# Moving 32 of 128 column copies from GpSimd to ScalarE ahead of its first silu of the last stage, and GpSimd's first roots from column 96 to column 80

## The chip, the cores and the metric

One core of one Trainium2 chip runs the whole program. The metric is device time in microseconds (us) of one execution. The kernel before takes 555.73 us (median of three runs, 555.04 to 556.38). The execution that was profiled took 554.09 us; its trace spans 552.1 us.

Engines in the rows: PE is TensorE's matmul, PEld its weight load, DVE is VectorE, ACT is ScalarE, POOL is GpSimd, SP is SyncE; a q behind a name is the sequencer of that engine, which handles registers, loads and waits.

## The reference

`x` is (64, 64, 256), 4096 tokens of 256 features. Two layers are applied and the result is added to `x`.

```python
# layer 1: mixture of 4 experts with a shared one, over all tokens c = L0(x, cond)
h = gelu(context_c @ ew1[e] + eb1[e]);  y = h @ ew2[e] + eb2[e]
out = out + w_be[:, e] * mask[e] * y          # plus the shared expert
# layer 2, on c, called x here
x1 = x @ sw1.T + sb1;  x2 = x @ sw2.T + sb2
sh = _ln(silu(x1) * x2, s_ln_g, s_ln_b)       # over H = 128
shared_out = sh @ sw3.T + sb3                 # all 4096 tokens
x_moe = x[index_b, index_t]                   # 512 selected positions
expert_scores = sigmoid(x_moe @ eg_w.T + eg_b)
top1_idx = argmax(expert_scores + exp_bias)
h1, h2 = x_moe @ ew1[e] + eb1[e], x_moe @ ew2[e] + eb2[e]     # 8 experts
z = _ln(silu(h1) * h2, sel_ln_g, sel_ln_b)
final_out = shared_out.at[index_b, index_t].set(shared_w * shared_out[...] + expert_w * expert_out)
```

The indices name fewer than 128 distinct tokens here, so they fit into one group, and only that group is worked on.

## The kernel before

**Layer 1** fills the first 480 us and keeps PE busy. Its sums lie in SBUF in `acc`, features in the partitions, a token in a column (two halves of 128 features, so a token is 128 partitions by 2 elements). When the last sum is written, VectorE raises `summed_all` (at 479.6 us in the trace).

**The last stage** (functions `stage2_*`) works through eight pieces of 512 tokens, k = 0 to 7, and one group of 128 selected tokens, the "group" below. Per piece:

- ScalarE `c_high(k)`: the sums cast to fp16 (L505). VectorE `c_low(k)`: the rest of them (L751).
- PE `first(k)`: 12 matmuls, x1 and x2 (L614). ScalarE `silu(k)` (L511), VectorE `gated(k)` (L758), ScalarE `g_high(k)` (L525), VectorE `g_low(k)` (L763).
- PE `centre(k)`: takes the mean off (L627). ScalarE `square(k)`: sums of squares (L517), which raises `sq_ready`.
- the root 1/sqrt(variance + eps): for pieces 0 to 3 on GpSimd, two pieces at a time, `roots(0)` and `roots(1)`, 15 dependent small operations each (L972 to L979), which raise `var_taken`. `roots(0)` waits for `square(1)`, `roots(1)` for `square(3)`.
- PE `second(k)`: the product with sw3 (L640). VectorE `rows(k)`: scales it by the root and adds x (L778); it waits for `var_taken` and raises `row_done`.

PE's order is first(0), a last part of layer 1 (`output_late(1)`, 487.73 to 493.13 us), then first(k), centre(k-1), and from k = 4 on second(k-4). `second(1)` waits for both halves of `rows(0)`, since they read the banks that it writes.

**The group.** GpSimd copies 128 columns of `acc`, chosen by a table of indices in SBUF (`ctab`), to `cgT`: one load of 16 registers, then 16 copies of 128x2 elements (`copies`, L947), eight times. The first three loads are done ahead of `summed_all`. The first of `roots` stands between column 95 and column 96, the second behind column 127. The last copy raises `cg_pool`. PE waits for it in `router(0)` (L647), which stands behind first(6), and runs the group's first matmuls (`gfirst`, L656) behind that.

Each engine runs its own list in the order written; semaphores tie them together. Nothing is reordered at run time.

Of the kernel before, what the change touches and what calls it, by code (L numbers as in the profile page):

```python
# [29 lines left out]
ACT = mybir.ActivationFunctionType  # L30
# [3 lines left out]
P = 128  # L34
# [25 lines left out]
COLS = NB * BS + SLOTS * SEG + 6  # L60
# [5 lines left out]
ROUND = 12582912.0  # L66
NJ = FE + 1
NL = 2
WARM = 11
NS1 = NS - NL  # L70
MGX = MG + 1
# [13 lines left out]
def program(nc, a):  # L85
    with ExitStack() as ctx:
# [3 lines left out]
        def sem(name):  # L90
            return ctx.enter_context(nc.semaphore(name))
# [229 lines left out]
        def take(base, lo, shape, dt=F32):  # L321

            n = 1
            for s in shape:
                n *= s
            words = n if dt is not F16 else n // 2
            v = base[:, lo:lo + words]
            if dt is not F32:
                v = v.bitcast(dt)
            names = "abc"[:len(shape)]  # L330
            if len(shape) == 1:
                return v
            return v.rearrange(f"p ({' '.join(names)}) -> p {' '.join(names)}",
                               **{c: s for c, s in zip(names, shape)})
# [8 lines left out]
        cgT = take(SW, 9216, [DB, P])  # L343
# [12 lines left out]
        ctab = stf[0:1, 0:MX].bitcast(I32)  # L356
# [25 lines left out]
        misc_in, w3s_in, ce8_in, xg_in = sem("misc_in"), sem("w3s_in"), sem("ce8_in"), sem("xg_in")  # L382
# [5 lines left out]
        var_taken, gvar_taken = sem("var_taken"), sem("gvar_taken")  # L388
        u_done, row_done, out_done, scat_done = sem("u_done"), sem("row_done"), sem("out_done"), sem("scat_done")

        cg_pool, fwr_in, late_done = sem("cg_pool"), sem("fwr_in"), sem("late_done")
        root_made, groot_made, root_step = sem("root_made"), sem("groot_made"), sem("root_step")
        logit_ready = sem("logit_ready")
# [38 lines left out]
        def halves(k, part):  # L432
            return chl[:, k % CR, part * DB:(part + 1) * DB, :].rearrange("p d (b t) -> p d b t", t=NT)

        def column(at):
            return acc[:, :, bass.ds(at, 1)]
# [61 lines left out]
        def stage2_act(act):  # L498

            def c_high(k):  # L500
                if k == NQ - 1:
                    act.wait_ge(late_done, 2)
                if k >= CR:
                    act.wait_ge(ab_done[1], k - CR + 1)
                nc.scalar.activation(halves(k, 0), summed(k), ACT.Copy).then_inc(c_hi, 1)  # L505
# [52 lines left out]
            def groot(g):  # L558
                act.wait_ge(gvar_taken, g + 1)
                nc.scalar.activation(tmg, tmg, ACT.Sqrt).then_inc(groot_made, 1)  # L560

            act.wait_ge(summed_all, 1)
            c_high(0)
            c_high(1)
            for k in range(NQ):
                silu(k)
                if k + 2 < NQ:
                    c_high(k + 2)
                if k == 6:
                    gsilu(0, 0)  # L570
                if k >= 1:
                    square(k - 1)
                g_high(k)
                if k == 6:
                    gsilu(0, 1)
                    score(0)
                    gsilu(0, 2)
                    gsilu(0, 3)
                if k == 7:
                    mix(0)  # L580
                    gsilu(0, 4)
# [19 lines left out]
        def stage2_pe(pe, output_late):  # L601
# [41 lines left out]

            def router(g):
                pe.wait_ge(cg_pool, g + 1)
                for db in range(DB):
                    pe.matmul(ps1[2][:, P:P + 9], cgT[:, db, :], rwr[:, db, :],  # L647
                              start=(db == 0), stop=(db == DB - 1))
# [282 lines left out]
        def stage2_pool(pool, link):  # L931
            pool.wait_ge(rows_ready, 1)
            link(nc.gpsimd.tensor_scalar(Cm32, ident[:, :], -1.0 / FH, None, ALU.add))
            link(nc.gpsimd.tensor_copy(Cm, Cm32))
            nc.gpsimd.memset(epss, EPS * WS * WS)
            nc.gpsimd.iota(io8, pattern=[[1, FE]], base=-FE, channel_multiplier=0,
                           allow_small_or_imprecise_dtypes=True).then_inc(const2_ready, 1)
            regs = [pool.alloc_register(f"pool_column{j}") for j in range(48)]
            groups = pool.value_load(tab[0:1, NR * ROW + 2:NR * ROW + 3], min_val=1, max_val=MGX)

            def addresses(g, at, j):
                pool.load(regs[j:j + 16], ctab[0:1, g * P + at:g * P + at + 16])  # L942
                return [pool.snap(x, min_val=0, max_val=COLS - 1) for x in regs[j:j + 16]]

            def copies(at, cols):
                for j, col in enumerate(cols):
                    i = nc.gpsimd.tensor_copy(cgT[:, :, at + j:at + j + 1], column(col))  # L947
                return i

            def x_rows(g):  # L950
                nc.gpsimd.indirect_dma_start(
                    out=xg, out_offset=None, in_=a["xR"],
                    in_offset=bass.IndirectOffsetOnAxis(ap=gid[:, g:g + 1], axis=0)).then_inc(xg_in, 16)

            def gather(g):
                x_rows(g)
                for at in range(0, P, 16):
                    i = copies(at, addresses(g, at, 0))
                i.then_inc(cg_pool, 1)

            def roots(q):
                taken = [q * 14]

                def link(i):
                    taken[0] += 1
                    i.then_inc(root_step, 1)
                    pool.wait_ge(root_step, taken[0])

                pool.wait_ge(sq_ready, 2 * q + 2)
                two = slice(2 * q * MG, (2 * q + 2) * MG)  # L970
                out = rstd[:, two]
                link(nc.gpsimd.tensor_scalar(tms, sums2[:, two], 1.0 / FH, EPS, ALU.mult, ALU.add))  # L972
                link(nc.gpsimd.tensor_scalar(out.bitcast(I32), tms.bitcast(I32), -0.5, MAGIC, ALU.mult, ALU.add))
                for n in range(3):
                    link(nc.gpsimd.tensor_tensor(qms, out, out, ALU.mult))
                    link(nc.gpsimd.tensor_tensor(qms, qms, tms, ALU.mult))
                    link(nc.gpsimd.tensor_scalar(qms, qms, -0.5, 1.5, ALU.mult, ALU.add))
                    link(nc.gpsimd.tensor_tensor(out, qms, out, ALU.mult))
                nc.gpsimd.tensor_scalar(out, out, 1.0 / WS, None, ALU.mult).then_inc(var_taken, 1)  # L979

            def scatter(g):

                pool.wait_ge(moe_ready, g + 1)
                nc.gpsimd.indirect_dma_start(
                    out=a["out"], out_offset=bass.IndirectOffsetOnAxis(ap=sid[:, g:g + 1], axis=0),
                    in_=moe, in_offset=None, bounds_check=TOK - 1, oob_is_err=False).then_inc(scat_done, 16)
                pool.wait_ge(scat_done, 16 * (g + 1))

            def group_in_front():
                pool.wait_ge(misc_in, 4 * 16)  # L990
                ahead = [addresses(0, at, at) for at in (0, 16, 32)]
                pool.wait_ge(summed_all, 1)
                for n in range(3):
                    copies(n * 16, ahead[n])
                for at in range(48, P, 16):
                    if at == 96:
                        roots(0)
                    i = copies(at, addresses(0, at, 0))
                i.then_inc(cg_pool, 1)
                roots(1)  # L1000
                x_rows(0)
                pool.wait_ge(out_done, 16 * NH)
                scatter(0)

            def groups_behind(g):
                gather(g)
                scatter(g)
                if g + 1 < MGX:
                    with pool.If(groups > g + 1):
                        groups_behind(g + 1)  # L1010

            with pool.If(groups > 1):
                group_in_front()
                groups_behind(1)
            with pool.If(groups < 2):
                group_in_front()
# [178 lines left out]
        def _(pe):  # L1195
# [48 lines left out]
            pe.wait_ge(zeros_ready, 1)  # L1244
            for n in range(WARM):
                pe.matmul(pst[:, :], zeros[:, 0:P], zeros, start=True, stop=True)
# [149 lines left out]
            def hidden_late(n):  # L1396
                at = 1 + TOK - (NL - n) * CH
                hidden(late + n, SH, lambda xp, db: X[:, 2 * xp + db, at:at + CH])
# [12 lines left out]
        def _(dve):  # L1411
# [376 lines left out]
            def late_store(n):  # L1788

                dve.wait_ge(y_done, last + (R0 + 2 + n))  # L1790
                at = NB - (NL - n) * CB
                for db in range(DB):
# [160 lines left out]
```

## Time and profile before

| | us |
|---|---|
| median of three runs | 555.73 (555.04 to 556.38) |
| profiled execution | 554.09 |
| its span in the trace | 552.1 |
| PE busy | 539.6 (98% of the span) |
| VectorE busy | 396.9 |
| ScalarE busy | 261.9 |
| GpSimd busy | 177.3 |

The busy share says that PE is the engine to look at; it doesn't say where PE waits. The chain of work that ended last is followed back from the last instruction; where it leaves PE for another engine, PE was waiting. The list of waits names for a stretch who waited for whom. The timeline shows an engine's work in order, with the idle time ahead of a piece in brackets and what ended it.

### The profile page before, as it was taken

Reading aid. Unit: us, or ns where it says so; the run is one execution under the profiler, and the core shown is the slowest. Engines: PE = TensorE matmul, PEld = TensorE weight load, DVE = VectorE, ACT = ScalarE, POOL = GpSimd, SP = SyncE. Lnnn points to the kernel's source line nnn. Section 1 sums busy time; section 2 is a strip of 40 time slices with the busy share of each in tenths; the row PEclk is TensorE's granted clock in tenths of the full one; section 3 lists DMA queues with packets and bytes.
Section 4 is the critical chain, followed back from the end, with each engine's and each line's share of the span. In section 5 each row is a group of like instructions: output and inputs, shape, how many; then the busy total and the mean of one; then the engine's idle time right before and its main releaser. Section 6 shows DMA issues by size and latency. Waiting matters only on the chain.

```text
span 552.1 us, 16532 instructions
## 1 busy us (share of the span) xinstructions
PE 539.6 (98%) x5082; PEld 481.1 (87%) x5083; DVE 396.9 (72%) x1046; ACT 261.9 (47%) x632; POOL 177.3 (32%) x566
## 2 busy tenths in 40 slices
PE   8999999999999999999999999999999999999895
PEld 5888888886889999999999999999999999865774
DVE  5979988674975757677675684887786645767585
ACT  6665766751434444343443433434424434539470
POOL 0280000000464523535335243342242410298700
PEclk9999999999999999999999999999999999999999
DMA  7722245300100002323310000000000000192233
GB/s 262 257 113 67 86 152 152 96 2 4 37 1 3 2 2 78 116 79 119 113 78 3 2 2 1 3 2 2 3 4 3 2 5 4 47 365 80 87 121 115
DMA packets 28476, 36.88 MB, mean 67 GB/s; under 512 B 4762, under 2 KB 24115, under 8 KB 28132
## 3 DMA queue, kind: packets, MB, share of 16 engines
q1 hardware_dynamic: 28292, 35.57, 19.6%
q8 instruction: 47, 0.77, 0.6%
q14 instruction: 41, 0.34, 0.2%
q0 software_dynamic: 96, 0.20, 0.1%
HBM read 27.30 MB, written 8.53 MB: 65 GB/s over the span
## 4 chain that ended last, share of the span: by engine, by line
PE 87%; POOL 4%; issue 3%; DVE 2%; POOLq 1%; DMA 1%; SPq 1%; ACT 0%; DVEq 0%; ACTq 0%
PE ps_out L1240 41%; PE ps_hidden L1210 40%; POOL W L947 2%; PE ps_hidden L656 2%; DMA W<-in_xT 1%; PE ps_out L1289 1%; DVE hbuf L1444 1%; PE ps_turn L640 0%; POOLq L942 0%; PE ps_hidden L640 0%; SPq L1021 0%; PE ps_small L640 0%; PE ps_hidden L614 0%; DVE W L1427 0%; PE ps_out L678 0%
## 5 line engine op out<-in xcount | busy, mean ns | idle before, releaser
L1240 PE MATMUL ps_out<-hbuf,W 128*128 128x242 f16 (+4 forms) x2304 | 242.9, 266 | 0.5 <-DVE W L1427 0.5
L1240 PEld LDWEIGHTS ps_out<-hbuf,W 128*128 (+1 forms) x2304 | 218.3, 98 | 17.5 <-DVE W L1427 0.8
L1074 ACT ACTIVATE h<-ps_hidden,b 128x242 f32<-128x242 f32 (+3 forms) x384 | 151.9, 462 | 67.3 <-PE ps_hidden L1210 64.5
L1882 POOL COPY xs<-X 128x88 f16 x334 | 111.1, 381 | 174.6 <-PE ps_hidden L1210 169.4
L1210 PE MATMUL ps_hidden<-xs,W 128*128 128x242 f16 (+2 forms) x1536 | 156.1, 262 | 1.1 <-issue 1.1
L1210 PEld LDWEIGHTS ps_hidden<-xs,W 128*128 (+1 forms) x1536 | 143.3, 98 | 9.3 <-issue 1.6
L1444 DVE TENSOR_TENSOR hbuf<-h,hbuf 128x484 f16<-128x484 f32 (+4 forms) x192 | 127.5, 664 | 7.5
L1735 DVE SCALAR_TENSOR_TENSOR acc<-ytmp,wrow,acc 128x44 f32 (+1 forms) x334 | 62.9, 260 | 80.5 <-ACT ytmp L1164 69.4
L1442 DVE CAST hbuf<-h 128x484 f16<-128x484 f32 (+4 forms) x192 | 83.8, 436 | 13.9 <-ACT h L1074 12.7
L1210 PE MATMUL ps_hidden<-X,W 128*128 128x256 f16 (+1 forms) x768 | 87.1, 273 | 0.9 <-DVE W L1427 0.8
L1164 ACT ACTIVATE ytmp<-ps_out,b 128x242 f32<-128x242 f32 (+3 forms) x64 | 25.5, 450 | 124.2 <-PE ps_out L1240 124.2
L1210 PEld LDWEIGHTS ps_hidden<-X,W 128*128 128x128 f16 x768 | 74.8, 98 | 11.0 <-DVE W L1427 1.6
L947 POOL COPY W<-acc 128x2 f32 x128 | 26.8, 274 | 37.9 <-DVE f L1803 35.3
L1858 POOL CAST ytmp<-tab 1x385 f32<-1x385 int32 x1 | 0.6, 631 | 102.1 <-DVE tab L1608 102.1
L1083 ACT ACTIVATE acc<-ps_out,b 128x256 f32<-128x256 f32 x28 | 11.7, 469 | 39.8 <-PE ps_out L1240 39.8
L1093 ACT ACTIVATE W<-stage 128x1024 f16<-128x1024 f32 x16 | 17.0, 1061 | 14.5 <-DMA stage<-in_ew 14.5
L1450 DVE SCALAR_TENSOR_TENSOR W<-stage,W 128x1024 f16<-128x1024 f32 x16 | 19.2, 1220 | 5.3 <-ACT W L1093 5.2
L614 PE MATMUL ps_hidden<-W,F 128*128 128x512 f16 x96 | 22.2, 379 | 0.2 <-DVE W L751 0.2
L614 PEld LDWEIGHTS ps_hidden<-W,F 128*128 128x128 f16 x96 | 9.2, 98 | 10.0 <-DVE W L751 0.7
L511 ACT ACTIVATE W<-ps_hidden,fb 128x512 f32<-128x512 f32 x8 | 5.6, 694 | 10.6 <-PE ps_hidden L614 10.6
L1466 DVE TENSOR_REDUCE acc<-W 128x16 f32<-128x336 f32 (+1 forms) x24 | 10.3, 499 | 0.0
L517 ACT ACTIVATE W<-ps_out 128x128 f32<-128x128 f32 x32 | 8.4, 277 | 3.1 <-PE ps_out L627 2.9
(316 smaller groups left out, 298.4 us busy)
## 6 DMA issues: line engine op xcount, KB each, us to landing
stage<-in_ew SPq DMA_DIRECT2D x16, 512.0 KB, 3.9
stage<-in_xR SPq DMA_DIRECT2D x8, 512.0 KB, 3.9
moved_rows<-stage SPq DMA_DIRECT2D x8, 512.0 KB, 2.6
X<-moved_rows SPq DMA_DIRECT2D x8, 512.0 KB, 10.1
out_rows<-X SPq DMA_DIRECT2D x16, 256.0 KB, 2.2
W<-in_xT SPq DMA_DIRECT2D x7, 512.0 KB, 9.3
W<-in_fw SPq DMA_DIRECT2D x1, 2304.0 KB, 11.6
W<-in_sw SPq DMA_DIRECT2D x4, 256.0 KB, 3.6
```

Of the source, the lines that this page charges most:

```text
L614: mm = pe.matmul(ps1[which][:, :], fw(wp, which, db), chl[:, k % CR, 2 * xp + db, :], start=(n == 0), stop=(n == 5))
L947: i = nc.gpsimd.tensor_copy(cgT[:, :, at + j:at + j + 1], column(col))
L1074: i = nc.scalar.activation(h32[:, j, k * size:(k + 1) * size], ps1[j][:, k * size:(k + 1) * size], ACT.Gelu_apprx_tanh, bias=b1[:, bass.ds ...
L1093: nc.scalar.activation(W[:, bass.ds(e * WE + at, 1024)], stage[:, k % 2, :], ACT.Copy, scale=WS).then_inc(hi_ready, 1)
L1164: i = nc.scalar.activation(ytmp[:, bass.ds(parity, 1), db, 0:size].rearrange("p o c -> p (o c)"), psy2[:, bass.ds(parity, 1), db * size:(d ...
L1210: mm = pe.matmul(out, w1(e, wp, db, hb), rhs(xp, db), start=(n == 0), stop=(n == 5))
L1240: mm = pe.matmul(out, w2(e, wp, hb, db), h, start=(n == 0), stop=(n == 3 * HB - 1))
L1442: nc.vector.tensor_copy(hi, src).then_inc(h_hi, 1)
L1444: nc.vector.tensor_tensor(lo, src, hi, ALU.subtract).then_inc(h_ready, 1)
L1450: nc.vector.scalar_tensor_tensor(W[:, bass.ds(e * WE + (at + 2048), 1024)], stage[:, k % 2, :], WS, W[:, bass.ds(e * WE + at, 1024)], ALU. ...
L1735: i = nc.vector.scalar_tensor_tensor(at, y, wrow[:, bass.ds(weight + j, 1)], at, ALU.mult, ALU.add)
L1882: i = nc.gpsimd.tensor_copy(xs[:, parity, :, j * SEG:(j + 1) * SEG], X[:, :, bass.ds(cols[j], SEG)])
```

## The change

ScalarE gets two blocks behind `c_high(1)` and ahead of `silu(0)`: each loads 16 indices to registers and copies 16 columns, 96 to 127 in all; the last copy raises a new semaphore `cg_act`. PE's `router` waits for it too. GpSimd's loop ends at column 95, and `roots(0)` stands ahead of column 80 instead of 96.

```diff
+ACOLS = 32
+        cg_act = sem("cg_act")
@@ stage2_act
+            act.wait_ge(misc_in, 4 * 16)
+            cols = [act.alloc_register(f"act_column{j}") for j in range(16)]
             act.wait_ge(summed_all, 1)
             c_high(0)
             c_high(1)
+            for at in range(P - ACOLS, P, 16):
+                act.load(cols, ctab[0:1, at:at + 16])
+                for j, x in enumerate(cols):
+                    col = act.snap(x, min_val=0, max_val=COLS - 1)
+                    i = nc.scalar.activation(cgT[:, :, at + j:at + j + 1], column(col), ACT.Copy)
+            i.then_inc(cg_act, 1)
             for k in range(NQ):
                 silu(k)
@@ stage2_pe, router(g)
                 pe.wait_ge(cg_pool, g + 1)
+                pe.wait_ge(cg_act, 1)
@@ stage2_pool, group_in_front
-                for at in range(48, P, 16):
-                    if at == 96:
+                for at in range(48, P - ACOLS, 16):
+                    if at == 80:
                         roots(0)
                     i = copies(at, addresses(0, at, 0))
                 i.then_inc(cg_pool, 1)
```

ScalarE before, at the start of the last stage: L505 is `c_high`, L511 `silu`, L525 `g_high`.

```order
L505 ACTIVATE W<-acc 128x1024 [waits summed_all]
L505 ACTIVATE W<-acc 128x1024
L511 ACT_TABLE_LOAD
L511 ACTIVATE W<-ps_hidden,fb 128x512 [waits a_done]
L505 ACTIVATE W<-acc 128x1024
L525 ACTIVATE W<-W 128x512 [waits g_made]
```

ScalarE now, at the same place: L507 is `c_high`, L570 the load of 16 registers, L572 a register operation, L573 the copy of a column, L513 `silu`.

```order
L507 ACTIVATE W<-acc 128x1024
L570 TENSOR_LOAD stage
L572 ISA
L573 ACTIVATE W<-acc 128x2
...
L570 TENSOR_LOAD stage
L572 ISA
L573 ACTIVATE W<-acc 128x2
...
L573 ACTIVATE W<-acc 128x2
L513 ACT_TABLE_LOAD
L513 ACTIVATE W<-ps_hidden,fb 128x512 [waits a_done]
```

Two loads and 32 copies stand between `c_high(1)` and the table load of `silu(0)`, which were neighbours.

GpSimd before, from column 80 to the second roots: L942 is the load of 16 registers, L947 the copy, L972 to L979 a set of roots.

```order
L942 TENSOR_LOAD stage
L943 ISA x2
L947 COPY W<-acc 128x2
...
L972 TENSOR_SCALAR stage<-stage 128x8 [waits sq_ready]
L973 TENSOR_SCALAR stage<-stage 128x8 [waits root_step]
...
L979 TENSOR_SCALAR stage<-stage 128x8 [waits root_step]
L942 TENSOR_LOAD stage
...
L942 TENSOR_LOAD stage
...
L972 TENSOR_SCALAR stage<-stage 128x8 [waits sq_ready]
```

GpSimd now, from column 64 to the second roots: L953 is the load, L958 the copy, L983 to L990 a set of roots.

```order
L953 TENSOR_LOAD stage
L954 ISA x2
L958 COPY W<-acc 128x2
...
L983 TENSOR_SCALAR stage<-stage 128x8 [waits sq_ready]
L984 TENSOR_SCALAR stage<-stage 128x8 [waits root_step]
...
L990 TENSOR_SCALAR stage<-stage 128x8 [waits root_step]
L953 TENSOR_LOAD stage
...
L983 TENSOR_SCALAR stage<-stage 128x8 [waits sq_ready]
```

The first roots come 16 columns sooner, and one load with 16 copies stands between the two sets of roots instead of two loads with 32.

## Rows read from the trace of the kernel before

**Rows 1.** The page: TensorE's granted clock in 40 slices; the chain that ended last, by engine.

```profile
PEclk9999999999999999999999999999999999999999
PE 87%; POOL 4%; issue 3%; DVE 2%; POOLq 1%; DMA 1%; SPq 1%; ACT 0%; DVEq 0%; ACTq 0%
```

**Rows 2.** Waits, 484 to 520 us: who waited for whom; us in total, times, longest.

```profile
DVE X L778 <- POOL stage L979: 1.7, 1, 1.7
...
PE ps_turn L640 <- DVE X L778: 1.4, 1, 1.4
...
PE ps_hidden L647 <- POOL W L947: 1.0, 1, 1.0
```

**Rows 3.** Timeline of PE: start, us, engine, line, operation, out<-in, count, idle before.

```profile
495.56 0.61 PE L627 MATMUL ps_out<-stage,W 128*128 128x128 f16 x8
...
509.22 0.61 PE L627 MATMUL ps_out<-stage,W 128*128 128x128 f16 x8
511.28 0.83 PE L640 MATMUL ps_turn<-V,W 128*128 128x256 f16 x6 [1.45 <-DVE X L778]
...
516.37 0.58 PE L647 MATMUL ps_hidden<-stage,W 128*128 128x9 f32 x4 [1.01 <-POOL W L947]
```

**Rows 4.** Timeline of POOL, from column 64 to the end of the second roots.

```profile
495.37 6.99 POOL L947 COPY W<-acc 128x2 f32 x32 [1.20 <-issue]
...
502.72 1.19 POOL L973 TENSOR_SCALAR stage<-stage 128x8 int32<-128x8 int32 x1
...
509.18 0.24 POOL L979 TENSOR_SCALAR stage<-stage 128x8 f32<-128x8 f32 x1
510.69 5.54 POOL L947 COPY W<-acc 128x2 f32 x32 [1.27 <-issue]
...
520.25 0.23 POOL L979 TENSOR_SCALAR stage<-stage 128x8 f32<-128x8 f32 x1
```

**Rows 5.** Timeline of ACT at the start of the last stage, and the end of square(1).

```profile
480.44 2.00 ACT L505 ACTIVATE W<-acc 128x1024 f16<-128x1024 f32 x2
482.46 1.28 ACT L511 ACT_TABLE_LOAD   x1
486.63 0.69 ACT L511 ACTIVATE W<-ps_hidden,fb 128x512 f32<-128x512 f32 x1 [2.89 <-PE ps_hidden L614]
...
494.46 0.69 ACT L511 ACTIVATE W<-ps_hidden,fb 128x512 f32<-128x512 f32 x1 [5.03 <-PE ps_hidden L614]
...
500.23 0.22 ACT L517 ACTIVATION_READ_ACCUMULATOR W<-ps_out 128x1 f32 x1
```

**Rows 6.** Groups by line and shape, ACT: count, busy us, mean ns, idle before.

```profile
L505 ACT ACTIVATE W<-acc 128x1024 f16<-128x1024 f32 x8 | 8.4, 1061 | 0.0
...
L555 ACT ACTIVATE stage<-stage 128x8 f32<-128x8 f32 x2 | 0.6, 312 | 0.0
...
L541 ACT ACTIVATE stage<-stage 128x1 f32<-128x1 f32 x1 | 0.2, 188 | 0.0
```

**Rows 7.** Timeline of ACT in layer 1: a pair whose addresses come from registers.

```profile
455.34 0.82 ACT L1074 ACTIVATE h<-ps_hidden,b 128x242 f32<-128x242 f32 x2 [0.42 <-PE ps_hidden L1210]
```

**Rows 8.** Timeline of POOL, one block of 16 copies that nothing holds up.

```profile
492.16 2.02 POOL L947 COPY W<-acc 128x2 f32 x16
```

**Rows 9.** By line, register loads: 16 values on POOL, one on ACT; ns min/median/max.

```profile
L942 POOLq TENSOR_LOAD <-stage x8: 1049/1056/1341, 447.5 to 512.4; - x8
L1156 ACTq TENSOR_LOAD <-tab x5: 272/277/279, 444.4 to 469.3; - x5
```

**Rows 10.** Timeline of DVE: the late store, a c_low, a g_low, rows(0).

```profile
493.26 0.76 DVE L1795 SCALAR_TENSOR_TENSOR acc<-ps_out,acc 128x256 f32<-128x256 f32 x2 [2.74 <-PE ps_out L1240]
...
502.63 1.22 DVE L751 TENSOR_TENSOR W<-acc,W 128x1024 f16<-128x1024 f32 x1
...
507.22 0.69 DVE L763 SCALAR_TENSOR_TENSOR W<-W 128x512 f16<-128x512 f32 x1 [0.26 <-ACT W L525]
509.56 0.88 DVE L778 SCALAR_TENSOR_TENSOR X<-ps_turn,stage,X 128x256 f32<-128x256 f32 x2 [1.66 <-POOL stage L979]
```

**Rows 11.** Copies of GpSimd (L947) in a stretch: its length, busy us and count.

```profile
479.70:498.80 19.10, 17.68 (x80) 1.00 0.94 330
```

## The prediction

> **What bounds the kernel now.** I read the chain that ended last first. It is PE for 87% of the span, at a full granted clock in every slice [rows 1], so what counts is where PE stands still in the last stage. The waits of that stretch come second: PE is idle twice for other engines, 1.4 us ahead of second(1), for rows(0), and 1.0 us ahead of the router, for GpSimd's copies; rows(0) itself waited 1.7 us for the roots [rows 2]. Third, the timelines say how the two hang together. PE has issued centre(4) by about 509.8 and starts second(1) at 511.28, idle 1.45; it starts the router at 516.37, idle 1.01 [rows 3]. GpSimd copies columns 64 to 95 until 502.36, works on the first roots until 509.42, waits 1.27 us for a register load, copies 96 to 127 until 516.23, and PE goes on 0.14 us later [rows 4]. So GpSimd sets PE's pace twice in the stretch from 509.8 to 516.4, by 2.46 us in all. ScalarE has its idle time elsewhere: 2.89 us ahead of silu(0) and 5.03 us ahead of silu(1), since PE is busy with the last part of layer 1 there [rows 5].
>
> **What the 32 copies cost ScalarE.** No row shows a 128x2 ACTIVATE. Bounds per copy: the shortest one, 128x1, takes 0.188 us, and two c_highs take 2.00 us where one takes 1.061, so neighbours overlap by 0.12; that leaves 0.07 us of spacing at best. The other end is an ACTIVATE of 128x8 at 0.312 with no overlap [rows 5, 6]. Register addresses don't forbid overlap: a pair of 242 columns with such addresses takes 0.82 us together [rows 7]. GpSimd's 16 copies, with the same register operation between them, take 2.02 us; less the last one's 0.19 that is 0.122 each, a rate set by its sequencer [rows 8]. ScalarE's sequencer has the same pairs to issue, so I take 0.12: 32 x 0.12 = 3.9 us, between 2.2 and 10.0.
>
> Register loads: 16 values take 1.056 us on GpSimd, one value 0.277 on ScalarE [rows 9]; a block of GpSimd that isn't ahead of its load idles 1.20 us [rows 4]. The first load of ScalarE can run under c_high(0) and (1), which need no sequencer; the second is exposed. I take 1.2 us, between 0 and 2.5. Sum: 5.1 us, between 2.2 and 12.5.
>
> ScalarE is free for them at about 482.4 [rows 5]. They end at 487.5; the table load of 1.28 us comes behind them and no longer beside the wait, so silu(0) starts at 488.8 instead of 486.63, 2.2 us late.
>
> What is queued behind: c_high(2), done 1.64 us after silu(0) starts; then on VectorE c_low(2), 1.22, g_low(0), 0.69, and the late store, 0.76 [rows 10]. That is 4.4 us, and PE wants the last two for centre(0) at 495.56 [rows 3]. So silu(0) may start as late as 491.1 at no cost. With 488.8 there are 2.3 us to spare; silu(1) at 494.46 waits for PE as before. If that cover were gone, each microsecond would count in full, because from then on square, g_high, g_low and centre wait for each other in turn. Cost taken: 0.
>
> A rule of the Trainium skill speaks against this step. "ScalarE: Activation LUTs", section "Rules for kernel authors", budgets about 0.3 us for each ACTIVATE; 32 would be 9.6 us, and silu(0) at 494.5, past the limit. The same page, section "What ACT_TABLE_LOAD costs", gives 186 ns for one with immediate scale and bias and an overlap of 93 ns, so some 3.0 us for 32. The 0.188 us row agrees with the second.
>
> **What it gives GpSimd.** 80 columns are copied by 498.80 [rows 11]. Then the roots wait for square(1), whose last read ends at 500.45 [rows 5], so they start at 500.5 instead of 502.4: 1.9 us sooner and not 3.5. They took 7.06 us (502.36 to 509.42); the second set took 4.25 us (516.23 to 520.48) [rows 4]. The difference is VectorE: while c_low runs from 502.63, one small operation takes 1.19 us instead of 0.2 [rows 4, 10]. The Trainium skill has this as a lock on a shared port pair ("SBUF — State Buffer", section "Who interferes with whom"); the trace agrees, and by the same rule ScalarE's copies are never held up. The new stretch holds the same VectorE work, so I take the blocked length: 507.5. The g_low from 507.22 to 507.91 would catch the last operation, so I take 508.0. Bounds: 504.8 and 509.0.
>
> rows(0) stands behind that g_low in VectorE's list, so it can't start ahead of 507.9 whatever the roots do. With 508.0 plus the 0.14 us between the roots' end and its start before, it starts at 508.1 instead of 509.56, and second(1) 1.72 us behind it as now: 509.83. PE is there at the same time. The 1.45 us go; nothing replaces them, since g_low and rows(0) end just in time.
>
> Then the router. PE arrives 1.45 us sooner, about 513.9. GpSimd has 16 columns left: roots until 508.0, a load of 1.27, 16 x 0.122 = 2.0, one c_low in the way (1.1): 512.4. The new semaphore of ScalarE was raised at 487.5. So the 1.01 us go too, with 1.5 us to spare. What else does PE need there? gated(5) and c_low(7) stand behind rows(0) and move with it: gated(5) ends near 510.6, c_low(7) near 511.8, and rows(1) and gated(6), the next to be wanted, by 514.8; the work that waits for them on PE comes behind the router. roots(1), at 520.48 now, comes to 512.4 plus 4.3 to 7, well ahead of rows(2). From the router on all engines follow PE, and the chain to the end is PE's and the last additions' behind it.
>
> **The sum.** 1.45 + 1.01 = 2.46 us against the profiled execution: 554.09 - 2.5 = 551.6. That execution is 1.6 us under the median of the runs shown; against the median it is 555.73 - 2.5 = 553.2. From here on I count against the median.
>
> **Rivals.**
>
> - *The roots are stalled longer.* GpSimd's ops land against one more c_low (1.1 us) and end at 509.0. Then rows(0) starts at 509.1, and only 0.4 of the 1.45 go; with the 1.01 of the router that is 1.5 us: 554.2. For it: four of the 15 operations were stretched before, by 2.8 us. Against it: the start is 1.9 us sooner and the VectorE work is as before.
> - *The gain is taken up behind the router.* ScalarE reloads tables and VectorE has its longest list around 522 to 529 us. If one of them, not PE, ends last there, PE waits later what it didn't wait sooner: 0 to 1 us gained, about 555.3. Against it: after 516.37 PE has no gap for another engine in the chain until second(7).
> - *ScalarE's copies are late (slower).* If each takes 0.312 us without overlap and both loads are exposed, the block is 12.5 us; silu(0) starts at 496.2, 5.1 us past 491.1. All of it goes into centre(0) and the chain behind, square(1) and the roots too: +5.1 - 2.46 = +2.6, 558.4. The point from which it decides: 9.9 us for the block (0.27 per copy with one load exposed) makes the time slower than before; between 7.4 and 9.9 it eats from the gain. For it: no row shows such short ACTIVATEs in a row with register work between. Against it: 128x1 at 0.188 and the pair at 0.82. The budget of 0.3 us in the Trainium skill's ScalarE page is this rival: silu(0) would be 3.4 us past the limit, 0.9 us slower than before.
>
> **How the numbers follow.** Chances: forecast 0.68, longer roots 0.13, taken up later 0.10, late copies 0.09. The measurement can tell about 0.2%, 1.1 us, from no change. The forecast's own range is 552.3 to 554.2. Faster by over 1.1 us: most of the forecast (0.65) and of the longer roots (0.10), 0.75. Within: the taken-up case, the rest of both and a sliver of late copies, 0.17. Slower: 0.08. The range takes in the roots' upper bound and the first part of late copies: 551.9 to 555.6.
>
> **What the profile of the changed kernel would show.** No idle time ahead of L640 at second(1), nor ahead of the router's matmuls. 32 ACTIVATEs of 128x2 at some 0.12 us of spacing, a gap of 1.2 us in their middle, silu(0) near 488.8 and silu(1) still near 494.5. GpSimd idle from 498.9 to 500.5, the first roots ended by 508.0, rows(0) close behind, the last copy near 512.4. The prediction is wrong if silu(0) starts after 491.1, if the roots end after 508.5, or if PE shows a new wait behind the router.

## The result, and the profile after

The changed kernel takes 552.47 us (median of ten, 551.32 to 553.50), the kernel before 555.43 us in the runs beside them. The ratio is 0.9953, 95% interval 0.9940 to 0.9966: 2.6 us faster. The profiled execution took 551.52 us with a span of 549.6 us, 2.5 us under the one before. Forecast were 553.2 us and 2.5 us.

The page's clock row and the chain that ended last, as in [rows 1]:

```profile
PEclk9999999999999999999999999999999999999998
PE 94%; DVE 2%; issue 1%; DMA 1%; SPq 1%; POOL 0%; ACT 0%; ACTq 0%; DVEq 0%; POOLq 0%
```

GpSimd had 4% of the chain and has left it. The waits from 484 to 520 us, where [rows 2] had PE waiting 1.4 and 1.0 us and rows(0) 1.7 us:

```profile
POOL stage L983 <- ACT W L519: 4.1, 1, 4.1
...
DVE X L789 <- POOL stage L990: 0.2, 1, 0.2
...
PEld ps_turn L650 <- DVE X L789: 0.2, 1, 0.2
```

No wait of PE's matmuls on rows(0) or on GpSimd is left; GpSimd itself waits now, for square(1). PE's timeline, against [rows 3]: the start of first(0), then centre(0), centre(4), second(1) and the router.

```profile
484.88 1.03 PE L624 MATMUL ps_hidden<-W,F 128*128 128x512 f16 x4
...
495.69 0.61 PE L637 MATMUL ps_out<-stage,W 128*128 128x128 f16 x8
...
509.33 0.61 PE L637 MATMUL ps_out<-stage,W 128*128 128x128 f16 x8
509.97 0.83 PE L650 MATMUL ps_turn<-V,W 128*128 128x256 f16 x6
...
513.88 0.51 PE L658 MATMUL ps_hidden<-stage,W 128*128 128x9 f32 x4
```

Neither second(1) nor the router has idle time in brackets. The start of the last stage differs by some tenths from one execution to the next (first(0) at 484.75 before, 484.88 here, up to 486.45 in a run below), so from here on places are counted from the start of first(0). Second(1) came at 26.53 and comes at 25.09, 1.44 us sooner; the router at 31.62 and at 29.00, 2.62 us sooner. That is 0.16 us more than the two waits: the router starts just ahead of the modelled end of first(6) now (513.88 for 511.29 + 2.75). From the router to PE's last matmul it is 29.60 and 29.52 us: behind the router nothing was given back.

ScalarE, against [rows 5]:

```profile
480.57 2.00 ACT L507 ACTIVATE W<-acc 128x1024 f16<-128x1024 f32 x2
482.47 1.61 ACT L573 ACTIVATE W<-acc 128x2 f32 x16
484.47 1.78 ACT L573 ACTIVATE W<-acc 128x2 f32 x16 [0.39 <-issue]
486.27 1.28 ACT L513 ACT_TABLE_LOAD   x1
487.56 0.69 ACT L513 ACTIVATE W<-ps_hidden,fb 128x512 f32<-128x512 f32 x1
...
494.60 0.69 ACT L513 ACTIVATE W<-ps_hidden,fb 128x512 f32<-128x512 f32 x1 [4.88 <-PE ps_hidden L624]
```

The 32 copies take 3.8 us with both loads; silu(0) is 0.8 us later against first(0), and silu(1) waits for PE as ever. GpSimd, against [rows 4]: the last copies ahead of the roots, the start, two held-up operations and the end of the roots, and the last 16 copies.

```profile
494.90 1.66 POOL L958 COPY W<-acc 128x2 f32 x13 [0.20 <-issue]
500.67 0.26 POOL L983 TENSOR_SCALAR stage<-stage 128x8 f32<-128x8 f32 x1 [4.11 <-ACT W L519]
...
502.81 1.23 POOL L986 TENSOR_TENSOR stage<-stage 128x8 f32<-128x8 f32 x1
...
507.50 0.61 POOL L990 TENSOR_SCALAR stage<-stage 128x8 f32<-128x8 f32 x1
509.01 3.64 POOL L958 COPY W<-acc 128x2 f32 x16 [0.90 <-issue]
```

The roots end at 508.11 and the last copy at 512.65, 1.2 us ahead of the router. VectorE, against [rows 10]: the g_low that held up the last root, and rows(0).

```profile
507.32 0.69 DVE L774 SCALAR_TENSOR_TENSOR W<-W 128x512 f16<-128x512 f32 x1 [0.25 <-ACT W L527]
508.25 0.88 DVE L789 SCALAR_TENSOR_TENSOR X<-ps_turn,stage,X 128x256 f32<-128x256 f32 x2 [0.24 <-POOL stage L990]
```

### The profile page after: what moved, and what is told of

The parts are those of the page before. It is cut to its first block, busy times and chain, and to the rows that moved or that the text cites. A ratio compares the mean times of both kernels' runs of the same rounds, so it can differ in the third digit from the quotient of the medians.

```text
span 549.6 us, 16531 instructions
## 1 busy us (share of the span) xinstructions
PE 540.3 (98%) x5082; PEld 481.5 (88%) x5083; DVE 397.2 (72%) x1046; ACT 264.4 (48%) x664; POOL 168.5 (31%) x534
## 4 chain that ended last, share of the span: by engine, by line
PE 94%; DVE 2%; issue 1%; DMA 1%; SPq 1%; POOL 0%; ACT 0%; ACTq 0%; DVEq 0%; POOLq 0%
PE ps_out L1251 42%; PE ps_hidden L1221 41%; PE ps_hidden L624 4%; PE ps_hidden L667 2%; DMA W<-in_xT 1%; PE ps_turn L650 1%; PE ps_small L650 1%; PE ps_out L637 1%; PE ps_out L1300 1%; DVE hbuf L1455 1%; DVE hbuf L1453 1%; PE ps_hidden L650 0%; SPq L1032 0%; DVE W L1438 0%; PE ps_out L689 0%
## 5 line engine op out<-in xcount | busy, mean ns | idle before, releaser
L958 POOL COPY W<-acc 128x2 f32 x96 | 19.9, 268 | 36.6 <-DVE f L1814 35.4
L1094 ACT ACTIVATE acc<-ps_out,b 128x256 f32<-128x256 f32 x28 | 11.7, 469 | 39.6 <-PE ps_out L1251 39.6
L1485 DVE TENSOR_TENSOR X<-W,X 128x1024 f16<-128x1024 f32 x7 | 8.7, 1245 | 1.7 <-ACT X L1116 1.7
```

## The experiments

Theory A: PE waited twice on GpSimd, each wait with its own cause (the roots' place, the number of columns), and ScalarE's copies are free as long as silu(0) starts within 6.35 us of first(0) (491.1 less 484.75). Rival B: GpSimd was just overloaded, so any 32 columns less would do. Rival C: the earlier roots bring it all. The kernels, beside the kernel before on the same chip; places are us from first(0), each from one profiled execution; where it says "spell", TensorE ran at its lower level for 3.4 us near the end (last section).

| kernel | ratio (95%) | silu(0) | second(1) | router | router to last matmul |
|---|---|---|---|---|---|
| before | | 1.88 | 26.53 | 31.62 | 29.60 |
| changed, again (two chips) | 0.9942 (0.9921-0.9963); 0.9942 (0.9919-0.9964) | 2.69 | 25.12 | 29.03 | 29.52; 31.21, spell |
| copies only | 0.9964 (0.9950-0.9977) | 2.67 | 25.70 | 29.61 | 29.52 |
| roots only | 1.0074 (1.0059-1.0088) | 1.89 | 25.10 | 33.79 | 32.64 |
| each copy three times | 0.9985 (0.9972-0.9999) | 8.23 | 26.87 | 30.78 | 31.21, spell |
| each copy twice | 0.9961 (0.9942-0.9979) | 5.21 | 25.11 | 29.02 | 31.21, spell |
| 16 columns | 0.9971 (0.9955-0.9987) | 1.89 | 25.09 | 30.14 | 31.27, spell |
| 48 columns | 0.9971 (0.9956-0.9986) | 5.42 | 25.09 | 29.00 | 31.20, spell |
| roots at 64 | 0.9973 (0.9958-0.9987) | 2.70 | 25.11 | 29.94 | 29.60 |
| copies behind g_high(0) | 0.9954 (0.9937-0.9972) | 1.90 | 25.13 | 29.05 | 31.21, spell |
| delay only | 0.9981 (0.9968-0.9993) | 2.67 | 25.68 | 30.73 | 29.60 |
| roots only, idle time filled | 1.0059 (1.0041-1.0078) | 1.89 | 25.13 | 33.82 | 29.61 |

**The changed kernel again.** 

> The changed kernel itself, so that the other three are compared with it on one chip. Both theories: 2.5 us faster than before; PE starts second(1) about 1.3 to 1.45 us and the router about 2.5 us sooner.

By the ratio (0.9942) 3.2 us faster. Run once more on another chip:

> The changed kernel once more, as the measure for the other three on this chip: 2.6 us faster than before.

The ratio was 0.9942 again. Both intervals hold the 2.5. The other kernels ran in three sessions: copies only, roots only and three times beside the first of these two, the three last of the table beside the second; twice, 16 columns, 48 columns and roots at 64 have the kernel before beside them but not the changed one.

**Copies only.** The roots behind column 95, ScalarE takes 32 columns.

```diff
-                    if at == 80:
-                        roots(0)
                     i = copies(at, addresses(0, at, 0))
                 i.then_inc(cg_pool, 1)
+                roots(0)
```

> ScalarE takes 32 columns, but the first roots stay behind column 95 as before. Theory A (two separate waits of PE on GpSimd, each with its own cause): the roots start at 502.4, second(1) keeps its 1.45 us of waiting, the router's 1.0 us goes, since its copies end ahead of the roots: 1.0 us faster than before, 1.5 us behind the full change. Theory B (GpSimd is simply overloaded, and any 32 columns less bring the gain): 2.5 us faster. Theory C (the earlier roots bring it all): no change.

Gained 2.0 us by the ratio (0.9964, 1.3 to 2.8 us), between A (1.0) and B (2.5), and the interval doesn't rule B out. The trace does: PE still waits ahead of second(1), 0.61 us, and the router is as much later than in the changed kernel (29.61 for 29.00). It is not what A forecast either. The router's wait is gone, as A has it; but second(1) came 0.83 us sooner, which A did not have:

```profile
510.83 0.83 PE L650 MATMUL ps_turn<-V,W 128*128 128x256 f16 x6 [0.61 <-DVE X L789]
```

GpSimd's list up to column 95 is that of the kernel before, yet it was through 1.2 us sooner. The delay-only kernel below was made for that.

**Roots only.** `ACOLS = 0`, the roots at column 80, no `cg_act`.

> GpSimd copies all 128 columns, with the first roots at column 80; ScalarE copies none. Theory A: second(1) starts 1.4 us sooner, but 48 columns stand between the roots' end (508.1) and the router: 0.9 for the load, 48 x 0.122 = 5.9, another load of about 1.2 exposed, about 1.1 for a VectorE operation in the way, so the router starts near 517.5 and not at 516.4: 1 us slower than before (0.3 to 1.5). Theory C: 1.4 to 2.5 us faster.

4.1 us slower, not 1. The sign is A's, and C is out; second(1) is as early as in the full change. The router is late:

```profile
518.62 0.99 PE L656 MATMUL ps_hidden<-stage,W 128*128 128x9 f32 x4 [4.61 <-POOL W L956]
```

I had put it near 517.5. Behind the roots GpSimd took 5.80 us for the first 32 copies, with 1.9 us of being held up where I had taken 1.1, and a third register load took 1.5 us and left 1.69 us idle for an expected 1.2. So the router comes 2.2 us later than before (33.79 for 31.62). The other 3 us are in the last column of the table, 32.64 for 29.60 us, and go with the clock (below). The two make 5.2 us. The 4.1 is less, probably because 14 of the 23 executions of the kernel before beside it had, by their mean clock, a shorter spell of their own near the end (last section); against the other nine it is 5.1 us (559.35 for 554.26).

**ScalarE's limit.** Two kernels issue each of ScalarE's copies twice or three times, the extra ones to unused space (here for three).

```diff
                     i = nc.scalar.activation(cgT[:, :, at + j:at + j + 1], column(col), ACT.Copy)
+                    for m in range(2):
+                        u = 2 * ((at - P + ACOLS + j) * 2 + m)
+                        i = nc.scalar.activation(moe2[:, u:u + 2].rearrange("p (k o) -> p k o", o=1),
+                                                 column(col), ACT.Copy)
```

> The full change, and ScalarE issues each of its 32 copies three times, twice to unused space: the result is the same. 64 ACTIVATEs more at 0.10 to 0.105 us put silu(0) at 487.6 + 6.5 = 494.1. The prediction's limit is 491.1: theory A, all past it counts in full: 3.0 us slower than the changed kernel, 0.5 us slower than the one before. Rival: the 5 us of idle time ahead of silu(1) is all slack (limit 492.4 or later), so the cost is 1.7 us or less and it stays faster than before.

> As the full change, but each copy of ScalarE is issued twice, once to unused space. 32 ACTIVATEs more at 0.10 us put silu(0) at 487.6 + 3.3 = 490.9, just inside the limit of 491.1. Theory A: same time as the changed kernel, within 0.2 us. Rival (ScalarE's delay leaks into the stage at once): 3.3 us slower than the changed kernel.

Twice: silu(0) at 5.21, inside the limit, and second(1) and router to 0.02 us where the changed kernel has them; by the ratio 2.2 us under the kernel before (1.2 to 3.2), so the rival's 3.3 us of loss didn't come. Three times: silu(0) at 8.23, 1.88 us past the limit. ScalarE and PE there:

```profile
493.30 0.69 ACT L513 ACTIVATE W<-ps_hidden,fb 128x512 f32<-128x512 f32 x1
```

```profile
494.13 2.75 PE L628 MATMUL ps_hidden<-W,F 128*128 128x512 f16 x12 [0.68 <-ACT W L513]
497.64 0.61 PE L641 MATMUL ps_out<-stage,W 128*128 128x128 f16 x8 [0.76 <-DVE acc L1810]
```

centre(0) waits for the late store (L1810), as the prediction's chain has it, and all behind it is 1.75 to 1.78 us later. First(1) waits for silu(0) itself too, 0.68 us, which the prediction didn't have; that loss is a part of the 1.75 and not on top of it. Of the 1.88 us past the limit all but 0.1 us is paid; by the rival's limit (492.4, 7.65 us from first(0)) it would have been 0.6. By time the kernel is 0.8 us faster than the one before (0.1 to 1.6) and not 0.5 slower as expected: 96 copies took less than I had put, 9.3 us with both loads, so silu(0) came at 8.23 and not 9.2. On this chip the changed kernel was 3.2 us faster than before, so three times costs 2.4 us by the ratios, with 1.75 of it in the places above and a spell at the lower clock in more of its executions (8 of 12 for 2 of 6, by the mean clock; last section).

**Other shares and places.** 16 columns (`ACOLS = 16`), 48 columns (`ACOLS = 48`, the roots behind column 79), the roots at column 64.

> ScalarE takes 16 columns, GpSimd 112, the first roots at column 80. The roots gain is kept; 32 columns stand between the roots and the router. From 509.0, 32 copies took 5.5 us before, with one VectorE operation in the way: 514.6 to 515.0, and PE is there at 513.9. Theory A: 0.7 to 1.1 us of waiting at the router, so 1.4 to 1.9 us faster than before. Rival (16 columns are enough): 2.5 us faster.

> ScalarE takes 48 columns; GpSimd copies 80 and then has only the roots. silu(0) comes at 487.6 + 1.9 = 489.5, inside the limit. Theory A: PE has no wait on GpSimd left to lose, so the time is that of the full change, 2.5 us under before. Rival (fewer columns on GpSimd always help): faster still, 3 us or more under before.

> The full change with the first roots at column 64 instead of 80. Theory A: the roots wait for square(1) until 500.6 either way, so they end at 508.1 as now, and 32 columns instead of 16 stand behind them: the router waits 0.7 to 1.1 us; 1.4 to 1.9 us faster than before. Rival (sooner in GpSimd's list means sooner done): the roots end sooner than 508, and rows(0) with them.

A holds in the traces in all three: the router comes 1.14 and 0.94 us later than in the changed kernel with 32 columns behind the roots, and 48 columns on ScalarE leave it at 29.00. Silu(0) comes at 5.42 there, inside the limit but 0.8 us later than expected, since a third load left ScalarE idle for 0.95 us. With the roots at column 64 they wait for square(1), whatever stands behind them:

```profile
500.95 0.26 POOL L983 TENSOR_SCALAR stage<-stage 128x8 f32<-128x8 f32 x1 [6.49 <-ACT W L519]
```

By the ratios, 16 columns and roots at 64 are 1.6 and 1.5 us under before, as expected. That of 48 columns is 1.6 under before too, for an expected 2.5, with an interval of 0.8 to 2.4; it gives no sign that fewer columns on GpSimd help further. A part of the difference to 2.5 is the spell at the lower clock near the end (last section), which by the mean clock came in 7 of its 12 executions and in 10 of 33 of the kernel before: executions with like clocks are 1.9 us apart (0.997 and over) and 2.5 us (0.994 to 0.995).

**Copies behind g_high(0).** The same block moved into the loop, behind `g_high(k)` for k = 0.

> ScalarE's two loads and 32 copies stand behind g_high(0) instead of ahead of silu(0), that is in the 5 us in which it waits for PE ahead of silu(1). Theory A (only the sum of the work up to silu(1) counts): they take 3.8 us from about 489.4, silu(1) starts at 494.5 as ever, and the time is that of the changed kernel within 0.3 us. Rival (the place ahead of silu(0) matters): different by 0.5 us or more, by way of VectorE's c_low(2), which would come about 1 us sooner again and hold up GpSimd's copies as in the kernel before.

2.6 us faster than before, the changed kernel in the same session 3.2, with intervals that overlap; places as in the changed kernel within 0.05 us, so there is no effect of the place on PE. The 5 us are used up in it: the block ends at 496.51 and silu(1) starts right behind, 0.26 us later than before, counted from first(0). The rival's mechanism did come: c_low(2) is as early as in the kernel before, and GpSimd is through column 79 at 14.5 us behind first(0) for 11.7 in the changed kernel. It costs nothing, because the roots wait for square(1) even then, for 1.29 us.

**Delay only.** ScalarE's 32 copies go to unused space; GpSimd has its 128 columns and the roots at 96.

```diff
-                for at in range(48, P - ACOLS, 16):
-                    if at == 80:
+                for at in range(48, P, 16):
+                    if at == 96:
```

> ScalarE makes its two loads and 32 copies, but to unused space; GpSimd copies all 128 columns with the roots at column 96, as in the kernel before. Open is why the run with the copies moved and the roots left where they were gained about 2 us and not 1. Theory D: the shift of VectorE's c_low(2) and g_low(0) by ScalarE's delay lets GpSimd hide a register load; then GpSimd is through column 95 about 1.2 us sooner here too, second(1) starts 0.8 us sooner, and the time is 0.8 us under before. Rival: fewer columns on GpSimd were needed for it, and this kernel takes as long as before.

Theory D's times hold: useless work on ScalarE makes the kernel 1.1 us faster (0.4 to 1.8). Second(1) is 0.85 us sooner and the router 0.89. GpSimd's copies up to column 63 in the kernel before (the rest is in [rows 4]); then those of this kernel, in 80 and 16, and VectorE's c_low(3):

```profile
479.80 14.38 POOL L947 COPY W<-acc 128x2 f32 x64 [35.26 <-DVE f L1803]
```

```profile
481.48 16.37 POOL L960 COPY W<-acc 128x2 f32 x80 [35.95 <-DVE f L1816]
499.05 3.80 POOL L960 COPY W<-acc 128x2 f32 x16 [1.20 <-issue]
```

```profile
498.19 1.22 DVE L764 TENSOR_TENSOR W<-acc,W 128x1024 f16<-128x1024 f32 x1
```

In [rows 4] GpSimd stood idle for 1.20 us at column 64, for a load. Here it is through column 79 at 11.4 us behind first(0), where it took 14.1, and then stands idle as long, at column 80. So no idle time was saved: what is shorter is the copies' own time, 20.17 us for 96 (16.37 + 3.80) against 21.37 (14.38 + 6.99). The idle time, 497.85 to 499.05, now falls mostly beside c_low(3), and an operation of VectorE that runs while GpSimd stands idle doesn't hold it up. In the kernel before, the idle time at column 64 fell into a stretch in which VectorE stood idle too (494.18 to 495.37), and c_low(3) held up a copy for 1.19 us later.

What moved the idle time is ScalarE's delay: it moves silu(0), and with it VectorE's c_low(2) and g_low(0) by 0.4 to 0.5 us, so that they hold GpSimd up three columns further on (column 37 for 34). The load for columns 64 to 79 is then made 7.8 us behind first(0) instead of 9.1, and is over before GpSimd needs it. The traces agree on that. In the five with silu(0) at 1.9 (before, roots only, roots only filled, 16 columns, copies behind g_high(0)) GpSimd stands idle for 1.2 us at column 64; in none of the five with silu(0) at 2.7 that copy straight on past it (the changed kernel and its two repeats, copies only, delay only) does it. That the delay brings the gain is shown by this kernel; why a few columns decide when the load is made is read from the traces and not tested by itself.

**Idle time filled.** As roots only, with 20 matmuls ahead of the router whose result isn't used.

```diff
+                    for _ in range(20):
+                        pe.matmul(ps1[3][:, :], fw(0, 0, 0), chl[:, k % CR, 0, :], start=True, stop=True)
                     pe.wait_ge(fwr_in, 16)
                     router(0)
```

> The kernel with only the roots moved, in which PE stood idle for 4.8 us ahead of the router, then ran at the lower clock for 6.8 us and took 3.1 us more from the router to the end. Here 20 matmuls of 512 columns (0.216 us each, 4.3 us), whose result is not used, fill that idle time; the wait itself stays. Theory W (the lower clock follows from the idle time): the clock stays at the upper level, the router starts at 518.6 as before, and the time is 3.1 us under the 559.35 of that kernel, 0.5 to 1 us over the kernel before. Rival (the clock falls for another reason, or the 3.1 us come from the copies' lateness): 559 us again.

The windows of roots only, and then of this one: length, busy time (count) of PE, PEld, DVE, ACT and POOL, granted clock, share of the DMA engines and GB/s.

```profile
513.80:518.20 4.40, 0.21 (x1) 0.00 (x0) 0.84 (x2) 0.00 (x0) 2.71 (x23) 1.00 0.35 119
518.20:525.00 6.80, 6.38 (x31) 6.35 (x32) 0.43 (x2) 0.37 (x1) 4.50 (x19) 0.50 0.02 7
525.00:531.00 6.00, 6.00 (x55) 5.43 (x53) 2.78 (x7) 5.43 (x16) 0.00 (x0) 1.00 0.18 58
```

```profile
513.80:518.20 4.40, 4.40 (x22) 1.99 (x21) 1.93 (x4) 0.69 (x1) 2.71 (x23) 1.00 0.35 119
518.20:525.00 6.80, 6.50 (x58) 5.55 (x57) 0.43 (x2) 1.82 (x10) 5.38 (x28) 1.00 0.01 2
```

In the trace theory W holds: with PE busy ahead of the router the clock stays at 1.00, and from the router to the last matmul it is 29.61 us again, 3.03 less. The timed runs show little of it: 559.22 us, 3.3 us over before (2.3 to 4.3), where 0.5 to 1 us over before was expected. The expectation was too low by itself, since the router is still 2.2 us later than before. The rest is probably the other spell, near the end (last section): five of the six executions had a mean granted clock of 0.994 to 0.995, the mark of that shorter spell, and one, the profiled one, had 0.998 and took 557.44. Five of the six of roots only lie at 0.992 to 0.993, one at 0.994. The shorter spell costs 1.7 us, and 557.44 + 1.7 = 559.1 is what the five took (558.29 to 560.20). So the fill seems to have kept the longer spell away in all six and to have got the shorter one in five. That is an estimate: the five have no trace.

## Why the prediction was right

- **PE's two waits on GpSimd.** 2.46 us forecast, 2.62 measured from first(0). Moving either half alone leaves a wait: 0.61 at second(1) with the copies alone, 4.61 at the router with the roots alone. The two are not a sum of two gains: the copies alone gained 2.0 us and the roots alone lost 4.1.
- **ScalarE's 32 copies.** The block was mis-sized, 5.1 us for 3.8. Spacing was 0.094 us for the first 16 ((1.61 - 0.20) / 15), which were queued while c_high(1) ran, and 0.105 for the rest, against 0.12. The second load was charged with 1.2 us and cost 0.39, since the first 16 were still being worked off. Neither touched the time, with 2.3 us to spare by forecast and 3.7 measured (2.68 of 6.35). With that much room the zero cost was safe even with the block wrong by a third. The Trainium skill's budget of about 0.3 us per ACTIVATE ("ScalarE: Activation LUTs", "Rules for kernel authors") is for one whose bias is a pointer operand of 128x1, a condition that the prediction left out; these copies have none, so the rule was no rival here. For immediate scale and bias the same page, "What ACT_TABLE_LOAD costs", has 186 ns less an overlap of 93 ns, and the measured 0.094 agrees.
- **The limit of 491.1 for silu(0).** Right to about 0.1 us: no cost at 5.21, and 1.76 us at 8.23, which puts it at 6.47 if each microsecond past it counts in full. The sum had a slip: its four terms make 4.31 and not 4.4, so the limit was 491.25, 6.50 from first(0), closer still. The slower rival was thus priced rightly; it didn't come because an ACTIVATE of 128x2 is no 0.27 us.
- **The roots.** Forecast from 500.5 to 508.0, measured 500.67 to 508.11. Five of the 15 operations were held up, for four before, so taking the blocked length and one more operation was right. rows(0) at 508.25 for 508.1, second(1) at 509.97 for 509.83: 0.13 of both is the later start of the stage.
- **GpSimd's first 80 columns.** Put at 498.8 as in [rows 11], but done at 496.56. I had held GpSimd's timing ahead of the roots for untouched by ScalarE's delay; the delay-only kernel shows that it isn't. It cost the forecast nothing, since the roots wait for square(1) anyway (4.11 us of idle time for an expected 1.6), and that was luck: the prediction had no term for it. It does mean that the account of the gain is not complete. Of the 2.62 us at the router, 0.89 come with the delay alone, 1.12 more with the 32 columns off GpSimd (30.73 to 29.61), and the last 0.6 with the roots' place (29.61 to 29.00). All of what the copies-only kernel gained at second(1) belongs to the delay (25.70 for 25.68).
- **Behind the router.** Nothing taken up later, as forecast: 29.52 us for 29.60.

## What to carry to other kernels

When two waits of the busiest engine go back to one helper, work out for each what stands in the helper's list ahead of what is waited for; here the share (32 columns) and the place (column 80) had to change together to clear both waits: the share alone gained 2.0 us and left one, and the place alone lost 4.1 us. The engine to take the work is the one that waits for the busiest engine at that moment, and its limit is found by following the chain to the next thing the busiest engine wants, not from its own idle time (6.35 us here, and not the 7.65 at which silu(1) would be late). Once the busiest engine has no wait left in the stretch, more relief moves nothing (48 columns for 32). And a delay of one engine can shift what two others do to each other: useless work on ScalarE made this kernel 1.1 us faster.

## What the runs showed of the hardware

**A wait of PE can cost more than its length.** In roots only, after 4.6 us of idle time ahead of the router, TensorE ran at 1.2 GHz instead of 2.4 (granted clock 0.50) for 6.8 us, and from the router to the last matmul it took 3.0 us more. With the idle time filled it stayed at 2.4 in the one execution that has a trace. The waits of 1.0 to 1.5 us in the kernel before and of 0.97 us with 16 columns were not followed by a fall of the clock at the router.

**A lower level near the end, in some executions.** The stretch from 539.7 to 543.1 us in two executions of the changed kernel, the profiled ones of its two repeats. Columns as in the windows above. The first ran through at the upper level, the second did not:

```profile
539.70:543.10 3.40, 3.40 (x24) 2.92 (x23) 2.94 (x8) 0.00 (x0) 0.00 (x0) 1.00 0.14 45
```

```profile
539.70:543.10 3.40, 3.40 (x14) 2.31 (x13) 1.91 (x5) 0.00 (x0) 0.00 (x0) 0.50 0.23 79
```

PE is busy in both, and did the same ahead of it: 18 matmuls of one column each, which in the second end 0.9 us before the clock falls, then matmuls of 256. The spell costs 1.7 us (31.21 for 29.52 from the router to the last matmul). All six traces with it have a mean granted clock of 0.995, the seven with no spell at least 0.997, and roots only, with the longer one, 0.992. By that mark it is most of why executions of one kernel spread over 2 us: in the first ten executions the changed kernel took 551.8 us at 0.997 or more (median of six) and 553.0 us at 0.995 (of four); the kernel before, on the chip of the first repeat, took 554.3 us (of nine) and 556.0 us (of fourteen). In which executions it comes I can't tell from these runs.

**Short ACTIVATEs pass at 0.094 us each** where they were queued ahead, register addresses included (the first 16 of the changed kernel), and at 0.105 where the sequencer made an address between each two (the other 16): less than GpSimd's 0.122 for the same copy. The second 16 ran beside VectorE's c_low(0) and c_low(1) at that even pace, while single copies of GpSimd took up to 1.26 us beside the same operations.
